# First convolution taps on ScalarE, the value table written in two parts, and all key taps ahead

## What is computed

```
x  = x + conv_block(ln_c(x))          # ln_c: layer norm over the channels
t  = tokens(x);  t = t + ffn(ln_t(t)) # 3136 tokens per image, 96 channels
conv_block(x):
  value = dwconv3x3(x, w_v, stride 1) + b_v
  query = dwconv3x3(x, w_q, stride 1) + b_q
  key   = dwconv3x3(x, w_k, stride 2) + b_k
  off   = dwconv3x3(x, w_off1, stride 2) + b_off1
  off   = gelu(ln(off) * ln_g + ln_b);  offset = off @ w_off2      # 784 points
  pos   = tanh(offset + ref)
  v     = bilinear(value, pos)                                     # 4 neighbours
  out   = per head (12): (query^T key) * scale, times v            # linear, no softmax
  y     = w_out @ out
ffn: gates = top-2 of softmax(t @ gate_w + gate_b), 4 experts
     out = sum_e gate_e * (gelu(t @ w1_e + b1_e) @ w2_e + b2_e)
```

## Time and profile before

| | |
|---|---|
| median of 3 runs | 759.47 us |
| profiled execution, own time | 761.6 us |
| its span | 759.8 us |
| PE busy | 715.7 us (94%) |
| DVE busy | 582.7 us (77%) |
| ACT busy | 384.5 us (51%) |
| POOL busy | 219.2 us (29%) |

### The profile page before, as it was taken

The page is one execution under the profiler, slowest core; times in us unless marked ns, Lnnn a source line. Parts: engine busy times, 40 slices in busy tenths (PEclk is TensorE's granted clock), DMA queues, the critical chain, the costliest instruction groups (busy, mean ns, idle before and its releaser), DMA issues.

```text
span 759.8 us, 9620 instructions
## 1 busy us (share of the span) xinstructions
PE 715.7 (94%) x3186; PEld 501.7 (66%) x3186; DVE 582.7 (77%) x1511; ACT 384.5 (51%) x722; POOL 219.2 (29%) x184
## 2 busy tenths in 40 slices
PE   5797999799999999999999999999989999999996
PEld 5557666566676666566676666666655665788884
DVE  4886648889999948799999477899983366577774
ACT  2314112755455613744545417644533137899995
POOL 4001700012118710111168300221186112344443
PEclk9997899699999999999999999999999999999998
DMA  8006200034474530336553422344744301111111
GB/s 197 5 0 195 56 5 1 0 76 83 91 205 94 111 66 1 61 79 147 133 142 84 93 50 45 72 86 82 195 94 100 59 19 40 56 60 59 65 46 37
DMA packets 29697, 58.66 MB, mean 77 GB/s; under 512 B 6224, under 2 KB 20176, under 8 KB 29360
## 3 DMA queue, kind: packets, MB, share of 16 engines
q0 software_dynamic: 11584, 17.90, 15.2%
q1 hardware_dynamic: 14336, 32.59, 14.4%
q10 hardware_dynamic: 3728, 7.55, 3.1%
HBM read 30.30 MB, written 14.65 MB: 59 GB/s over the span
## 4 chain that ended last, share of the span: by engine, by line
PE 73%; DMA 8%; DVE 6%; ACT 6%; POOL 3%; issue 2%; ACTq 0%; POOLq 0%; DVEq 0%
PE py L744 17%; PE pd L660 8%; DMA xbuf<-ye 7%; PE ph L576 7%; PE ph L760 4%; PE ph L761 4%; PE ph L762 4%; PE pa L527 4%; PE pa L648 3%; PE pd L630 2%; PE ph L780 2%; PE ph L782 2%; PE ph L781 2%; PE py L792 2%; PE py L795 2%
## 5 line engine op out<-in xcount | busy, mean ns | idle before, releaser
L744 PE MATMUL py<-hid,w 128*96 128x448 f32 x504 | 235.3, 548 | 10.4 <-ACT hid L1002 7.9
L1002 ACT ACTIVATE hid<-ph,b 128x448 f32<-128x448 f32 x252 | 159.0, 632 | 149.8 <-PE ph L762 146.3
L1476 POOL DMA_DIRECT2D xbuf<-ye x76 | 67.6, 890 | 343.6 <-DMA xbuf<-ye 175.5
L760 PE MATMUL ph<-x_hi,w_hi 96*128 96x448 f32 x252 | 164.5, 653 | 0.0
L1465 POOL DMA_INDIRECT big<-value_table,rows x64 | 89.2, 1393 | 83.2 <-DVE rows L1189 56.9
L744 PEld LDWEIGHTS py<-hid,w 128*96 128x96 f32 x504 | 81.8, 165 | 30.0 <-ACT hid L1002 12.4
L761 PE MATMUL ph<-x_lo,w_hi 96*128 96x448 f32 x252 | 93.6, 371 | 0.0
L762 PE MATMUL ph<-x_hi,w_lo 96*128 96x448 f32 x252 | 93.1, 370 | 0.0
L1412 DVE SCALAR_TENSOR_TENSOR ye<-py,b,gate_all 96x448 f32<-96x448 f32 x112 | 75.5, 675 | 11.6 <-PE py L744 8.6
L1478 POOL TENSOR_TENSOR xbuf<-xbuf,ye 96x448 f32<-96x448 f32 x36 | 53.9, 1497 | 101.0 <-DVE ye L1412 98.3
L1439 DVE TENSOR_TENSOR hid_lo<-hid,hid_hi 128x448 fp32r<-128x448 f32 x84 | 59.7, 711 | 27.2 <-ACT hid L1011 27.0
(11 more groups left out here) (165 smaller groups left out, 1093.4 us busy)
## 6 DMA issues: line engine op xcount, KB each, us to landing
gate_all<-gate_rows SPq DMA_DIRECT2D x56, 336.0 KB, 3.5
xbuf<-ye POOLq DMA_DIRECT2D x76, 168.0 KB, 3.6
value_table<-valT ACTq DMA_DIRECT2D x6, 1176.0 KB, 8.1
out<-xbuf SPq DMA_DIRECT2D x28, 168.0 KB, 2.0
xbuf<-in_x SPq DMA_DIRECT2D x3, 1176.0 KB, 10.8
value_table<-valT SPq DMA_DIRECT2D x2, 672.0 KB, 5.4
big<-value_table,rows POOLq DMA_INDIRECT x64, 2.8
value_table<-valT SPq DMA_DIRECT2D x2, 504.0 KB, 6.8
```

Source lines behind the costliest of these rows:

```text
L744: nc.tensor.matmul(py[e % 2][0:C, 0:GPIX], w2[:, c, :], hid[:, k % 3, :], start=(j == 0), stop=(j == CPE - 1)).then_inc(hid_used, 1)
L760: nc.tensor.matmul(bank, w1_hi[:, cols], xh(b, g), start=True, stop=False)
L1002: nc.scalar.activation(hid[:, k % 3, :], ph[k % 2][:, 0:GPIX], ACT.Gelu, bias=b1[:, k % NCH:k % NCH + 1]).then_inc(hid_act, 1)
L1476: pool.dma_start(to, ye[0:C, e, :], accum_op=ALU.add).then_inc(ye_summed, 16)
```

## The change

1. Tap 0 of every convolution is done on ScalarE (`start_taps`): one activation Identity per block with the tap's weight as scale and the bias as bias. DVE's `tap` returns for k = 0; its tap 1 waits for a semaphore that ScalarE raises. In batch 0 the taps follow the padding; later they stand between gelus, at places that `GELUS_AHEAD` gives.
2. For batches 1 to 3 the value table is written in two parts, slots 0 to 3 and slots 4 to 6, each as soon as it is copied, by four DMAs on ScalarE's queue instead of two. (Batch 0 did that before, on SyncE's queue.)
3. In batch 0 all nine key taps stand ahead of the positions (before: four), the off transposes stand between value slots 3 and 4, and `x_to_tokens` of batch 1 is split: two slots before the query convolutions on PE, five after three of them.
4. The tables of numbers are new; most entries move by 0 to 2 chunks (valT of batches 1 and 3 and the pieces behind it by one).

```diff
-KEYS_AHEAD = 4
-VALUE_HALF = 4
+KEYS_AHEAD = 9
...
+            def start_taps(b, m, dst, stride, blocks, before=lambda i: None):
+                for i in blocks:
+                    before(i)
+                    nc.scalar.activation(dst[:, i, :].rearrange("c (h w) -> c h w", w=W // stride), xpad[:, i, 0:QH:stride, 0:W:stride],
+                                         ACT.Identity, bias=conv_b[:, m, i:i + 1], scale=conv_w[:, m, i, 0:1]).then_inc(first_tap[m], 1)
...
# DVE, tap
+                if k == 0:
+                    return
...
-                    if k == 0:
-                        tapped[(m, i)] = step(v.tensor_scalar(to, src, w, conv_b[:, m, i:i + 1], ALU.mult, ALU.add))
-                        continue
-                    need(tapped[(m, i)])
+                    if k == 1:
+                        dve.wait_ge(first_tap[m], first_taps_done(b, m, i))
+                    else:
+                        need(tapped[(m, i)])
...
# PE, first_rest
-                values_to_tokens(b)
+                values_to_tokens(b, slots=range(VALUE_HALF))
                 off_to_channels(b)
+                values_to_tokens(b, slots=range(VALUE_HALF, QT))
                 offsets(b)
-                x_to_tokens(b + 1)
+                x_to_tokens(b + 1, slots=range(EARLY_SLOTS))
                 pe.wait_ge(diag_ready, 4)
                 convolve(2)
                 to_samples(b, "keyT", key, key_conv, b + 1)
                 convolve(1)
+                x_to_tokens(b + 1, slots=range(EARLY_SLOTS, QT))
                 key_values(b, range(2))
...
# ACT, rest
-                values_to_tokens(b, lambda s: gelus_to(plan.act_at("valT", s)))
-                act.wait_ge(act_done, acted(b, "valT", QT - 1))
-                for start in (0, ODD_BASE * 2 * C - C):
-                    act.dma_start(flat[start:start + PIX * C].rearrange("(j p k) -> p j k", j=QUARTERS, p=TP),
-                                  valT[:, :, :, :].rearrange("p j s c -> p j (s c)")).then_inc(table_out, 16)
+                for start, end in ((0, VALUE_HALF), (VALUE_HALF, QT)):
+                    values_to_tokens(b, lambda s: gelus_to(plan.act_at("valT", s)), range(start, end))
+                    act.wait_ge(act_done, acted(b, "valT", end - 1))
+                    for row in (0, ODD_BASE * 2 * C - C):
+                        act.dma_start(flat[row:row + PIX * C].rearrange("(j p k) -> p j k", j=QUARTERS, p=TP)[:, :, start * C:end * C],
+                                      valT[:, :, start:end, :].rearrange("p j s c -> p j (s c)")).then_inc(table_out, 16)
```

One of the tables, with a line as an example:

```diff
-    dict(valT=(198, 198, 199, 199, 200, 200, 201), keyT=(204, 204), kv=(222, 226, 233, 233), mix=(233, 233, 234, 234),
+    dict(valT=(197, 197, 198, 198, 199, 199, 200), keyT=(203, 203), kv=(221, 225, 233, 233), mix=(233, 233, 234, 234),
```

More of the change, by code:

```diff
@@ L56 @@
 TABLE_ROWS = ODD_BASE + PAIRS
+EARLY_SLOTS, VALUE_HALF = 2, 4
 def jobs(b, name, number):
@@ L398, in build, with dve_blocks, blocks_of, first_taps_done @@
         VALUE_CONVS = 4
-        def dve_blocks(b):
-            return [2] if first(b) else range(BLOCKS)
+        def dve_blocks(b, m):
+            return [i for i in range(BLOCKS) if not (first(b) and (m, i, 0) in first_convs)]
+        def blocks_of(b, m):
+            return list(dve_blocks(b, m)) if m in (VALUE, QUERY) else list(range(BLOCKS))
+        def first_taps_done(b, m, i):
+            return sum(len(blocks_of(a, m)) for a in range(b)) + blocks_of(b, m).index(i) + 1
         flat = table.rearrange("r c -> (r c)")
@@ L510, in transposes, with x_to_tokens @@
                 return last
-            def x_to_tokens(b, before=lambda g: None):
-                for s in range(QT):
+            def x_to_tokens(b, before=lambda g: None, slots=range(QT)):
+                for s in slots:
                     before(s)
@@ L611, in head, with values_to_tokens @@
                 nc.tensor.matmul(py[0][0:C, 0:EXPERTS], mean_of, gate_w[:, :], start=True, stop=True).then_inc(gate_mean, 1)
-            def values_to_tokens(b, before=lambda s: None):
-                for s in range(QT):
+            def values_to_tokens(b, before=lambda s: None, slots=range(QT)):
+                for s in slots:
                     before(s)
@@ L898, in head @@
                 act.wait_ge(conv_in, 32)
+                act.wait_ge(act_done, acted(b, "pad", 2 * BLOCKS - 1))
+                start_taps(b, OFF, off, 2, blocks_of(b, OFF))
+                start_taps(b, VALUE, val, 1, blocks_of(b, VALUE))
+                start_taps(b, KEY, key, 2, blocks_of(b, KEY))
+                act.wait_ge(weights_split, 1)
+                start_taps(b, QUERY, query, 1, blocks_of(b, QUERY))
                 convolved(0, 3)
@@ L958, in first_rest @@
                 key_to_samples(b)
-                convolved(6, 8)
+                convolved(6, 7)
+                x_to_tokens(b + 1, slots=range(EARLY_SLOTS, QT))
+                convolved(7, 8)
                 mixes(b)
@@ L984, in rest @@
                 act.wait_ge(dve_done, dved(b, "kv", QUARTERS - 1))
+                if with_head:
+                    act.wait_ge(act_done, acted(b + 1, "pad", 2 * BLOCKS - 1))
+                    start_taps(b + 1, OFF, off, 2, range(BLOCKS), lambda i: gelus_to(plan.act_at("off0", i)))
                 for g in range(NG):
@@ L991, in rest @@
                 if with_head:
+                    start_taps(b + 1, QUERY, query, 1, range(BLOCKS), lambda i: gelus_to(plan.act_at("query0", i)))
                     next_offsets(b + 1, plan, gelus_to)
+                    start_taps(b + 1, KEY, key, 2, range(BLOCKS), lambda i: gelus_to(plan.act_at("key0", i)))
             def experts():
@@ L1131, in tap, with off_tap, key_tap @@
                         tapped[(m, i)] = step(ins)
-                    elif i == blocks[-1]:
+                    elif i == order[-1]:
                         ins.then_inc(ready, 1)
             tapped = {}
-            def off_tap(k):
-                tap(OFF, k, off, 2, off_conv, range(BLOCKS))
-            def key_tap(k):
-                tap(KEY, k, key, 2, key_conv, range(BLOCKS))
+            def off_tap(b, k):
+                tap(b, OFF, k, off, 2, off_conv, range(BLOCKS))
+            def key_tap(b, k):
+                tap(b, KEY, k, key, 2, key_conv, range(BLOCKS))
             def floor(dst, src, big, m=1.0):
```

76 lines of the change are left out of this document (44 added, 32 removed), and 24 rows, old and new, of tables (OUTPUTS_AHEAD, SUMS_AHEAD).

## The result

Twenty runs of each: the changed kernel takes 754.57 us (749.29 to 762.89), the kernel before 759.38 (755.92 to 763.25). The ratio is 0.9939 with the interval 0.9916 to 0.9963, that is 4.6 us less, between 2.8 and 6.4. Forecast were 752.3 and 7.2 us less. The profiled execution took 754.6 us (span 752.7), 7.0 less than the 761.6 of before, but that one stood 2.2 above its median and this one at its own.

What follows compares the result with a forecast made beforehand. PE, busy 715.7 of 759.8 us, was taken as the bound, so only its idle or half-clock time counts. Terms -3.8, -1.2, -4.5, +0.5, +0.8 and +1.0 sum to -7.2: median 752.3 us, range 745.5 to 760.5.

Steps and rivals of the forecast that it cites:

- batch 0's transposes: Batch 0 on PE: 40 transpose records moved behind the third convolution run at full instead of half clock, -3.8 us.
- Rival 3: PE is simply full: half of each gain is lost at the next wait, costs stay; about 758 us, chance 0.08.
- Batch 2's tanh, -1.2: Batch 2's positions: DVE loses six first taps, so ACT's 3.87 us and PE's 1.19 us waits go; range 0 to -1.2.
- Batch 3's gathers, -4.5: Batch 3: gathers start 4 to 5 us earlier, saving PE 4.5 of 6.3 us lost; range 0 to -6.3.
- First taps in batch 0's tokens, +0.5: Batch 0's token work: three taps ahead of `x_hi` on ACT don't fit its 0.86 us of idle time, +0.5 us.
- First taps between gelus, +0.8: Expert chunks on ACT: taps of 784 elements at 0.95 us cost PE about 0.2 per group, four groups, +0.8 us.
- the prediction's own rule: Between gelus: gelu plus tap exceed the 1.36 us chunk period; after three in a row, the excess over 0.5 slack costs PE.
- Table writes, +1.0: ScalarE's queue, batches 1 to 3: two more DMA issues per batch at 0.54 us, partly absorbed by slack, +1.0 us.
- the prediction's own signs of being wrong: Table DMA issue blocking ACT over 2 us in several batches, first gather's distance unchanged, or `hid` waits exceeding 7.9 by over 2.
- rival 4: ACT blocks on table DMA issues between valT slot 3 and the gelus, six pairs, 3.2 us each; about 767, chance 0.12.
- the prediction's 0.9: Table write by the skill's transfer costs: four halves 14.8 us against 13.9 for two wholes, landing 0.9 us later.
- rival 2: Batch 3's gathers do not start earlier because POOL's chain of sums sets them; about 756.8 us, chance 0.17.

Runs made afterwards that it cites:

- e8: Kernel before with only batch 1's transposes split, two slots ahead of and five behind the third of batch 0's convolutions: 753.99 us, ratio 0.9943.
- e2: Changed kernel with all 56 transposes of batch 1's image ahead of batch 0's convolutions again: 757.21 us, ratio 0.9991 to the kernel before.
- e5: Changed kernel again, unchanged, run and profiled a second time: 755.64 us, ratio 0.9978 to the kernel before.
- e1: Kernel before again, unchanged, profiled a second time: 757.95 us.
- e10: Kernel before with only the value table of batches 1 to 3 written in two parts: 756.46 us, ratio 0.9972.
- e3: Changed kernel with the value table of batches 1 to 3 written whole, two DMAs for four: 752.79 us, ratio 0.9917 to the kernel before.
- e11: Changed kernel with batch 2's sums as before and the table of batches 1 to 3 written whole: 750.65 us, ratio 0.9893 to the kernel before.
- e6: Changed kernel with the numbers of sums ahead of batch 2's gathers as before: 750.92 us, ratio 0.99 to the kernel before.
- e12: Kernel before with only batch 1's transposes split and the table in two parts; taps and number tables stay: 750.31 us, ratio 0.9901.
- e4: Changed kernel with first taps back on VectorE, all orders and tables kept: 758.95 us, ratio 0.9968 to the kernel before.

## Why the prediction was right, and where it was not

**The direction and the main term.** 3.8 us was forecast for batch 0's transposes. The account has 4.8 (3.3 to 5.5 over all profiles that have the split), e8 brings 4.3 by doing it alone, and e2, which undoes it, is at 0.9991 where the changed kernel is at 0.9939 and 0.9978. The mechanism is as told: the clock falls, the transposes don't bring it back, the convolutions do. The added taps were covered, with 0.90 us left of DVE's 5.42.

**The sum is nearer than its parts.** Forecast were gains of 9.5 us and costs of 2.3; the first two profiles show 15.6 and 8.7. That the net came out near 7 in these profiles, and at 4.6 over the medians, is in part luck: gains and losses were both too small, and the largest loss stood in no term. (Rival 3 was also summed 1 us too high: half of 9.5, less 2.3, is 2.45 below 759.47, so 757.0.)

**Batch 2's tanh, -1.2.** The account has -2.3: all of PE's lateness behind the positions went, not only the wait of 1.19 us that I named.

**Batch 3's gathers, -4.5.** The first gather came at 540.79, the last slot's issues at 531.39: 9.4 us where 14.2 were (11.6 in e5, 12.1 in e1). PE's loss fell by 6.0 us against the first profile, but by 3.2 against the second (e1). The term was read from one execution: the 1.6 us of half clock in the earlier trace rows isn't in every run. In the time it is not borne out. With the +1.0 for the writes, the table in two parts was to bring 3.5 us; it brings 1 to 2 alone (e10), and in the changed kernel nothing that shows (e3, and e11 against e6), since the blocked issues take it back.

**First taps in batch 0's tokens, +0.5.** This was right: 0.57. Before, `x_hi` began 1.92 us after the end of the last padding copy (139.75 to 141.67), now 2.49 us after it:

```profile
138.51 1.24 ACT L856 ACTIVATE xpad<-pa 128x504 f32<-128x504 f32 x2 [0.22 <-PE pa L532]
```

```profile
133.18 1.24 ACT L872 ACTIVATE xpad<-pa 128x504 f32<-128x504 f32 x2 [0.22 <-PE pa L546]
134.45 1.49 ACT L878 ACTIVATE kv_area<-xpad,conv_b,conv_w 128x196 f32<-128x196 f32 x3
...
136.91 0.52 ACT L957 ACTIVATE x_hi<-pd 96x448 fp32r<-96x448 f32 x1
```

Three taps took 1.49 us, and the 0.86 us of idle time in the earlier trace rows took up the larger part. The row of the account grew by more, 1.4 (11.4 for 10.0). The rest lies in the first chunks: the granted clock was back at 1.00 at 150.5 us, 6.1 us after PE's first second product began at 144.44, where before it was 4.9 us (154.1 and 149.22). That is worth 0.6.

**First taps between gelus, +0.8.** A tap of 784 elements takes 1.03 us, not 0.95, and yet less is lost:

```profile
316.21 1.03 ACT L878 ACTIVATE query<-xpad,conv_b,conv_w 128x784 f32<-128x784 f32 x1
317.14 0.62 ACT L1047 ACTIVATE hid<-ph,b 128x448 f32<-128x448 f32 x1
317.66 1.03 ACT L878 ACTIVATE query<-xpad,conv_b,conv_w 128x784 f32<-128x784 f32 x1
318.59 0.62 ACT L1047 ACTIVATE hid<-ph,b 128x448 f32<-128x448 f32 x1
```

Starts of gelus are 1.45 us apart, so 0.09 over the chunk's 1.36, since an instruction's end overlaps the start of the next on ScalarE: 1.03 + 0.62 is 1.65 in the rows and 1.45 in time. Over the groups behind batch 0's first chunks the account finds 0.2 us. The Trainium skill's cost for ScalarE ("ScalarE: Activation LUTs", What ACT_TABLE_LOAD costs) had given 1.03, to the hundredth. By the prediction's own rule 1.03 would have raised the sum by 0.8 to 1.0, not 0.6. The Trainium skill's advice to keep multiply and add on VectorE (rules for kernel authors; the page's own reason is VectorE's rate per element) agrees with the rows for one instruction, 1.03 us for 0.680. For the kernel's time it is neither borne out nor refuted, since moving the taps had no price and no worth that shows (e12 against e6).

**Table writes, +1.0.** In the first profile they cost 1.0 less than before (3.4 for 4.4), in e5 1.2 more (5.6). No issue of the first parts blocked; the last DMA of each batch did, by 1.7 to 2.1 us (3.12 for the pair in e5), where before only batch 2's had, by 2.9. At 2.06 and 2.05 us in batches 1 and 2 this meets one of the prediction's own signs of being wrong, an issue of over 2 us in more than one batch. It is rival 4's mechanism, at three places instead of six, and between gelus it costs less than the 3.2 us that I charged unless the clock falls behind it. The rule on large transfers ("DMA: Bandwidth & Descriptors" of the Trainium skill, bandwidth) would have had the split write land later, by its table an estimated 1.2 us rather than the prediction's 0.9. The split let the gathers start 1.4 to 3.5 us sooner after the last slot (10.7 for 12.1 and 14.2, e10).

**What was missing: batch 2's `key_values`, 2.5 to 9 us.** The step that failed is the one on the tables: I costed their shifts of one or two chunks at nothing. PE's `kv` pieces moved one chunk forward, the sums ahead of GpSimd's last gathers went from 44 to 46, and the gains ahead of it brought PE there some 7 us sooner still, while the gathers hang on the sums' landings. That was rival 2's mechanism, seen at batch 3 and not looked for in batch 2. e6 shows it by one line of numbers: without that stall the change brings the 7 us that were forecast (0.99, interval 0.9859 to 0.994), with it 4.6 and, in the second set, 1.7. This is the largest place where the gains of batches 0 and 3 went; the 1.6 us at batch 3's tokens is another that no term had.

**What stays open.** Why the same idle time is followed by half clock in one run and not in the next; why the last of four table issues blocks and the first three don't; and the own worth of first taps and new tables: e6 against e12 shows none, but can't see less than some 4 us; e11 against e8 points to 3.8 us gained, within the noise; and e4 takes the taps off tables that were drawn for them.

## What to carry to other kernels

Find where the busiest engine stands still or runs at half clock and put work that doesn't mind behind the work that restores the clock: one such move was worth as much as the whole of this change. When a gain moves one engine forward, follow it to the next place where that engine meets a chain that didn't move with it (here sums and gathers on GpSimd), and read its slack first. And profile the kernel before twice: a term that exists in one execution only is not there to be gained.

## What the runs showed of the hardware

- PE at the 1.2 GHz level (clock 0.51) did 10.75 us of back-to-back 96x96 transposes without its clock rising (before, e2), and was at 1.00 within 2 to 5 us of the start of 128x392 matmuls (changed kernel's first profile, e2).
- A wait of PE of 2.1 to 2.2 us was followed by a long stretch at half clock (0.54 over 15 us, e2), by a short fall (0.86 over 12 us, first profile) or by none (e5), in the same program or one that differs only in batch 0. A wait of 1.81 us at batch 3's tokens was followed by a fall in the changed kernel (0.93 over 26 us) and by none in the kernel before (1.00 over 634 to 640).
- Issuing a table DMA on ScalarE's queue takes 0.31 to 0.52 us, but the last of a batch's four took 1.7 to 2.1 us in the changed kernel's first profile, with the DMA engines at a share of 0.88 around batch 2's (1.2 to 3.0 us in all profiles with four).
- Identity with scale and bias on ScalarE: 1.03 us for 128x784; three of 128x196 in a row take 1.49.
